# A decoder layer's last batch attended in two halves of 256 tokens, with half of its routing beside the attention

## The reference

```python
def _relu_kernel(x, proj):                      # random features, M = 128
    return relu(einsum('blhd,md->blhm', x, proj) / sqrt(128)) + 1e-3
q, k, v = query @ Wq, source @ Wk, source @ Wv  # 16 heads of 64; source: 77 context tokens a batch
kvs = einsum('blhm,blhd->bhmd', kp, v)
num = einsum('blhm,bhmd->blhd', qp, kvs)
den = einsum('blhm,bhm->blh', qp, sum_l(kp))
att = num / den ; out = einsum('blhd,hdk->blk', att, Wo)
...
routing = softmax(xf @ router_w.T)              # 8 experts, the best 2 of each token
y = (silu(xf @ w_gate) * (xf @ w_up)) @ w_down  # hidden size 256
out = sum over the 2 of weight * y
```

## Time and profile before

| | |
|---|---|
| median of 3 runs | 296.51 us (294.48 to 297.17) |
| the profiled execution | 296.67 us, its span 294.9 us |
| mixer and folds | to about 108 us |
| attention (PE) | to 195.3 us |
| experts (PE) | 196.6 to about 280 us |
| busy | PE 84%, PEld 71%, DVE 62%, ACT 54%, POOL 37% |
[...]

### The profile page before, as it was taken

The page is one execution under the profiler, slowest core; times in us unless marked ns, Lnnn a source line. Parts: engine busy times, 40 slices in busy tenths (PEclk is TensorE's granted clock), DMA queues, the critical chain, the costliest instruction groups (busy, mean ns, idle before and its releaser), DMA issues.

```text
span 294.9 us, 5862 instructions
## 1 busy us (share of the span) xinstructions
PE 247.8 (84%) x1730; PEld 210.3 (71%) x1730; DVE 182.7 (62%) x721; ACT 158.2 (54%) x339; POOL 108.7 (37%) x161
## 2 busy tenths in 40 slices
PE   7799999999899999998999899859587777788800
PEld 3468786767789998996899688748576766777700
DVE  2867877878288878977796889687521212112206
ACT  3275565646677776776576766514444424345400
POOL 4388623402010010074006503614565655655520
PEclk9999999999999999999999999999999999999955
DMA  7899669999120000010001100537857885672147
GB/s 241 248 216 182 110 135 186 170 181 190 48 111 0 2 0 4 0 47 28 1 2 36 38 2 13 160 94 232 226 159 213 201 235 167 174 209 75 32 139 288
DMA packets 36254, 35.36 MB, mean 120 GB/s; under 512 B 3973, under 2 KB 27658, under 8 KB 36096
## 3 DMA queue, kind: packets, MB, share of 16 engines
q1 hardware_dynamic: 33520, 30.23, 44.6%
q0 software_dynamic: 2272, 4.24, 4.2%
q10 hardware_dynamic: 432, 0.52, 0.5%
HBM read 19.84 MB, written 14.32 MB: 116 GB/s over the span
## 4 chain that ended last, share of the span: by engine, by line
PE 64%; DVE 13%; issue 8%; DMA 5%; ACT 4%; POOL 2%; another core or an unknown queue 2%; SPq 1%; POOLq 0%; DVEq 0%; ACTq 0%
PE num L1455 15%; PE front L1559 9%; PE num L1569 5%; PE front L1399 5%; PE num L1377 4%; PE front L280 4%; PE front L282 3%; PE front L281 3%; DVE X L1033 3%; PE back L1341 2%; PE num L280 2%; PE back L1288 2%; DVE X L1279 2%; DVE hid L1247 2%
## 5 line engine op out<-in xcount | busy, mean ns | idle before, releaser
L1033 DVE SCALAR_TENSOR_TENSOR X<-num,rden,X 128x128 f32<-128x128 f32 x256 | 75.6, 342 | 4.8
L1455 PEld LDWEIGHTS num<-kvw_sb,q 128*128 128x128 f32 x512 | 66.7, 190 | 14.0 <-issue 5.7
L1455 PE MATMUL num<-kvw_sb,q 128*128 128x130 f32 x512 | 69.1, 277 | 6.1 <-DVE X L1033 5.7
L589 POOL DMA_INDIRECT dispatched<-rows,slot_i x32 | 31.3, 977 | 56.1 <-PE front L282 28.9
L744 ACT ACTIVATE relu_z<-front 128x512 f32<-128x512 f32 x64 | 38.1, 595 | 24.2 <-PE front L282 22.5
L1247 DVE TENSOR_TENSOR hid<-front,silu_g 128x256 f32<-128x256 f32 x39 | 16.5, 423 | 55.1 <-ACT silu_g L774 38.7
L624 POOL DMA_INDIRECT expert_out<-yo,xb x39 | 38.0, 975 | 32.0 <-ACT yo L778 19.4
L1559 PE MATMUL front<-xT,wgu_sb 128*128 128x128 f32 x312 | 41.8, 277 | 5.2 <-issue 3.6
L640 ACT ACTIVATE q<-relu_z 128x512 f32<-128x512 f32 x64 | 40.4, 632 | 5.9 <-PE num L1455 0.4
L1559 PEld LDWEIGHTS front<-xT,wgu_sb 128*128 128x128 f32 x312 | 37.9, 192 | 6.2 <-issue 6.2
L1569 PE MATMUL num<-wd_sb,hid 128*128 x156 | 25.8, 288 | 10.8 <-DVE hid L1247 9.4
(11 more groups left out here) (175 smaller groups left out, 382.2 us busy)
## 6 DMA issues: line engine op xcount, KB each, us to landing
wgu_sb<-in_wgu SPq DMA_DIRECT2D x39, 256.0 KB
dispatched<-pad_row SPq DMA_DIRECT2D x3, 2795.0 KB, 19.1
xb<-dispatched SPq DMA_DIRECT2D x39, 65.0 KB
y_back<-expert_out SPq DMA_DIRECT2D x4, 512.0 KB, 5.0
wd_sb<-in_wd SPq DMA_DIRECT2D x1, 1024.0 KB, 4.8
out<-X SPq DMA_DIRECT2D x4, 256.0 KB, 2.2
X<-in_x SPq DMA_DIRECT2D x3, 256.0 KB, 4.7
expert_out<-yo,xb POOLq DMA_INDIRECT x39
```

What stands on the lines that cost most here:

```text
L589: g.indirect_dma_start(out=xs, out_offset=bass.IndirectOffsetOnAxis(ap=slot_i[:, m % 2, t, k:k + 1], axis=0), in_=rows[:, m % 2, k, t, :], ...
L1033: ins = v.scalar_tensor_tensor(tile_of(n, t), banks[:, t // 2, t % 2, 0:P], rden[:, f % 2, t:t + 1], tile_of(n, t), ALU.mult, ALU.add)
L1455: last = nc.tensor.matmul(num[:, 2 * (h % 2) + t // 2, HA * (t % 2):HA * (t % 2 + 1)], q[:, h % 4, part], kvw_h, start=True, stop=True)
```

## The change

The last batch is worked in two halves of its tokens. A unit is now two heads for 256 tokens instead of one head for 512: `features` issues 3 matmuls of 256 columns for each of the two heads into the halves of the same bank, `numerators` uses the first head's keys for two tiles and the second's for the other two, and DVE adds both heads to the same two tiles, so that the third and fourth update of X wait for the first and second. After 8 units, tokens 0 to 255 have all their heads. Routing has five jobs now: batches 0 to 2 whole, and the two halves (`HALF_A`, `HALF_B`) of batch 3. The first half's routing is placed beside units 8 to 12 of the last batch on DVE, 11, 12 and 14 on PE, and 11, 14 and 15 on ACT; the second's stays between the first blocks of the experts, with half the tokens. The functions take slices of the tiles; counts of steps follow the width of the job (`routed`).

Scatters: `SPREAD` lists, for each batch in progress and job, the half heads at which one is issued. Batch 0 sends two in batch 1 and six in batch 2, four halves apart; batch 1 sends two in batch 2 and six in batch 3; batch 2 sends eight in batch 3 at halves 19 to 30, and the first half of the last batch four at 31, 33, 35 and 37. The experts keep four scatters, at gates 4 to 7, and with the last gate at 7 the sends of blocks 3 to 38 spread over 31 blocks instead of 28.

```diff
-        SCATTER_HEAD = (10, 13)
-        PACE = (0, 1, 3, 5, 6, 8, 9, 11)
+        SPREAD = {(1, 0): (26, 30), (2, 0): (2, 6, 10, 14, 18, 22), (2, 1): (26, 30), (3, 1): (1, 5, 9, 12, 15, 17),
+                  (3, 2): (19, 20, 22, 23, 25, 27, 28, 30), (3, 3): (31, 33, 35, 37)}
+        NORM_AT, HALF_NORM_AT = 2, 4
         BURST = 3
-        BURST_GATES = (4, 5, 6, 7, 7, 8, 9, 10)
+        BURST_GATES = (4, 5, 6, 7)
         HALVES = 2
         ACT_Y3, ACT_TWICE, ACT_SECOND = (5, 6), (5, 8), (8, 10)
         PE_Y3, PE_LOGITS, PE_RANKS = (5, 6), (6, 7), (8, 10)
         PE_SUMS, DVE_SUMS = 1, 3
         DVE_TABLE = (5, 3)
-        ROUTE_STEPS = 21
+        JOBS = [(m, 0, TPB) for m in range(NB - 1)] + [(NB - 1, 0, TPB // 2), (NB - 1, TPB // 2, TPB)]
+        HALF_A, HALF_B = NB - 1, NB
+        PE_HALF, ACT_HALF, DVE_HALF = (11, 12, 14), (11, 14, 15), 8
...
+        def heads_summed(r):
+
+            return (JOBS[r][0] + 1) * H - (H // 2 if r == HALF_A else 0)
...
-            def scatters(n, m):
-
-                first = 2 * SCATTER_HEAD[m < NB - 2]
-                for i in range(TOPK * TPB):
-                    after_head(n, first + PACE[i])
-                    scatter(m, i // TOPK, i % TOPK)
+            sent_of = [0] * len(JOBS)
+
+            def scatters(n, r, start=0, stop=None):
+
+                for half in SPREAD.get((n, r), ())[start:stop]:
+                    after_head(n, half)
+                    scatter(r, sent_of[r])
+                    sent_of[r] += 1
 
             for n in range(1, NB):
                 if n == 1:
                     ln2(NB - 1)
+                scatters(n, n - 2, 0, NORM_AT)
                 third_norm(n - 1)
-                scatters(n, n - 1)
-            third_norm(NB - 1)
+                scatters(n, n - 2, NORM_AT)
+                if n < NB - 1:
+                    scatters(n, n - 1)
+            scatters(NB - 1, NB - 2, 0, HALF_NORM_AT)
+            third_norm(HALF_A)
+            scatters(NB - 1, NB - 2, HALF_NORM_AT)
+            scatters(NB - 1, HALF_A)
+            third_norm(HALF_B)
 
             def last_scatters():
-                for i in range(TOPK * TPB):
+                for i in range(TOPK * width(HALF_B)):
                     pool.wait_ge(gu_full, BURST_GATES[i])
-                    scatter(NB - 1, i // TOPK, i % TOPK)
+                    scatter(HALF_B, i)
...
+            def turned_rows(r):
+                act.wait_ge(tb_full, r + 1)
+                copy(y3T[:, 0:P * width(r)], t_bank[:, 0:P * width(r)]).then_inc(y3T_done, 1)
...
+                        if k == ACT_HALF[0]:
+                            turned_rows(HALF_A)
+                        if k == ACT_HALF[1]:
+                            second_silu(HALF_A)
+                        if k == ACT_HALF[2]:
+                            second_rows(HALF_A)
...
-                    ins = v.scalar_tensor_tensor(tile_of(n, t), banks[:, t // 2, t % 2, 0:P], rden[:, f % 2, t:t + 1], tile_of(n, t),
+                    tile = tile_of(n, t if n < NB - 1 else 2 * (h // (H // 2)) + t % 2)
+                    if n == NB - 1 and t >= 2:
+                        dve.wait_ge(pair_step if t == 2 else att_done, h + 1 if t == 2 else f * HALVES + 1)
+                    ins = v.scalar_tensor_tensor(tile, banks[:, t // 2, t % 2, 0:P], rden[:, f % 2, t:t + 1], tile,
                                                  ALU.mult, ALU.add)
                     if t % 2:
                         ins.then_inc(att_done, 1)
-
...
+                    elif n == NB - 1 and t == 0:
+                        ins.then_inc(pair_step, 1)
...
+                if r >= HALF_A:
+                    dve.wait_ge(ln3_step, 2 * (r + 1))
+                    v.tensor_tensor(l_diff[:, part], l_diff[:, part], rstd[:, part], ALU.mult).then_inc(u_done, 1)
+                    dve.wait_ge(u_done, 2 * (r - HALF_A) + 2)
...
-                if (1, 2) <= (k, t) <= (2, 1):
-                    third_norm(m, TPB * k + t - TPB - 2)
+                if (1, 3) <= (k, t) <= (2, 2):
+                    third_norm(m, TPB * k + t - TPB - 3)
...
+                at = TPB * (k - DVE_HALF) + t
+                if at == 0:
+                    third_stats(HALF_A, 0)
+                    third_stats(HALF_A, 1)
+                if at == 1:
+                    third_moments(HALF_A, 0)
+                    third_moments(HALF_A, 1)
+                if at == 2:
+                    mean_share(HALF_A)
+                if at == 8:
+                    centred_logits(HALF_A)
+                    tops(HALF_A)
+                if at == 9:
+                    top_indices(HALF_A)
+                    top_number(HALF_A)
+                if at == 10:
+                    choose(HALF_A)
+                    take(HALF_A)
+                if at == 11:
+                    difference(HALF_A)
+                    never_zero(HALF_A)
+                if at == 12:
+                    inverse(HALF_A)
+                    third_norm(HALF_A, 0)
+                if at == 13:
+                    third_norm(HALF_A, 1)
+                if at == 16:
+                    slots(HALF_A)
+                    slots_chosen(HALF_A)
+                if at == 17:
+                    places(HALF_A)
+                    second_weight(HALF_A)
+                    counts(HALF_A)
+                if at == 18:
+                    first_weight(HALF_A)
+                    place_numbers(HALF_A)
...
+            def head_of(n, h, i):
+
+                return h if n < NB - 1 else 2 * (h % (H // 2)) + i
+
             def features(n, h):
                 wait_past(pe, relu_done, n * H + h - 1)
+                if n == NB - 1:
+                    tokens = slice(POS // 2 * (h // (H // 2)), POS // 2 * (h // (H // 2) + 1))
+                    for i in range(2):
+                        part = slice(M * head_of(n, h, i), M * (head_of(n, h, i) + 1))
+                        last = split_matmul(z_bank[h % 2][:, POS // 2 * i:POS // 2 * (i + 1)], feat_hi[:, part], feat_lo[:, part],
+                                            y2T_hi[:, n, tokens], y2T_lo[:, n, tokens])
+                    last.then_inc(z_full, 1)
+                    return
                 part = slice(M * h, M * (h + 1))
                 split_matmul(z_bank[h % 2], feat_hi[:, part], feat_lo[:, part], batch(y2T_hi, n), batch(y2T_lo, n)
                              ).then_inc(z_full, 1)
...
             def numerators(n, h):
                 f = n * H + h
                 pe.wait_ge(q_done, f + 1)
-                kvw_h = batch(kvw_sb[:, :, HA * h:HA * (h + 1)], n)
                 for t in range(TPB):
                     part = slice(P * t, P * (t + 1))
                     if t % 2 == 0:
                         wait_past(pe, att_done, (f - 2) * HALVES + t // 2 + 1)
-                    last = nc.tensor.matmul(num[:, 2 * (h % 2) + t // 2, HA * (t % 2):HA * (t % 2 + 1)], q[:, h % 4, part], kvw_h,
-                                            start=True, stop=True)
+                    at = head_of(n, h, t // 2)
+                    last = nc.tensor.matmul(num[:, 2 * (h % 2) + t // 2, HA * (t % 2):HA * (t % 2 + 1)], q[:, h % 4, part],
+                                            kvw_sb[:, n, HA * at:HA * (at + 1)], start=True, stop=True)
                 last.then_inc(num_done, 1)
...
+            def turn_last(r):
+
+                pe.wait_ge(att_done, heads_summed(r) * HALVES)
+                transposes(t_bank, [X[:, TPB * (NB - 1) + t, :] for t in range(*JOBS[r][1:])]).then_inc(tb_full, 1)
...
+                        if k == PE_HALF[0]:
+                            turn_last(HALF_A)
+                        if k == PE_HALF[1]:
+                            router_logits(HALF_A)
+                        if k == PE_HALF[2]:
+                            ranks(HALF_A)
...
-                    turn_last()
+                    turn_last(HALF_B)
                 if s == 1:
-                    router_logits(NB - 1)
+                    router_logits(HALF_B)
 
             pipeline(pe, [(0, turn_x), (1, gate_up), (1, behind_gate), (2, down)], next_experts, beside={
-                3: [lambda: ranks(NB - 1)]},
+                3: [lambda: ranks(HALF_B)]},
```

More of the change, by code:

```diff
@@ L326, in turned_x, with width, tiles_of, tiles_routed @@
             return (t_bank, o_bank)[s][:, 0:P] if s < 2 else tx_bank[j % 2][:, 0:P]
+        def width(r):
+            return JOBS[r][2] - JOBS[r][1]
+        def tiles_of(r):
+            return slice(JOBS[r][1], JOBS[r][2])
+        def tiles_routed(r):
+            return sum(width(j) for j in range(r + 1))
+        def heads_summed(r):
+            return (JOBS[r][0] + 1) * H - (H // 2 if r == HALF_A else 0)
+        def routed(r, step=None):
+            steps = [2 * width(j) + 13 for j in range(r + 1)]
+            if step is None:
+                return 1 + sum(steps)
+            return 1 + sum(steps[:r]) + (step if step == 0 else width(r) if step == TPB else step - 2 * TPB + 2 * width(r))
```

(23 more changed lines are left out.)

249 lines of the change are left out of this document (124 added, 125 removed).

## The result

The changed kernel takes 289.05 us (median of 4 runs, 286.90 to 289.92) where the kernel before takes 296.84 (4 runs, 294.48 to 299.05): a ratio of 0.9746, interval 0.9695 to 0.9798, so it is faster by 2.5%. The profiled execution took 288.63 us, its span is 286.9 against 294.9.

The account below looks back on a forecast made before the run. PE was taken to lead the chain, DVE to bound dense routing, with stalls from dense indirect DMAs. Terms -2.6 + 2.7 + 1.6 - 1.3 - 0.7 - 1.9 = -2.2 against 296.67 gave 294.5 us, range 288.5 to 300.5.

Parts of the forecast that it names:

- the sum: Whole kernel: all terms added, -2.2 us against the profiled execution, 294.5 us; chance 0.44 for 291.5 to 297.5.
- rival B: Experts: spacing pays there too, only the 5 blocks with doubled sends stall, -6.4 us, 290 us; chance 0.22.
- (b): Last batch: the first half's routing moves into DVE's attention work, 3.1 us of it against 0.44 idle: +2.7 us.
- (c): Last batch, POOL: twelve scatters at its minimum distance, priced at two stalls: +1.6 us, bounds -1.6 and +5.3.
- (d): Block 0 of the experts: batch 2's last scatter comes earlier, so PE's wait for `xb` goes: -1.3 us.
- (e): PE's routing between the first expert blocks halves: -0.7 us.
- (f): Experts: four scatters leave, at 0.46 us a DMA: -1.9 us, or 0 if only PE's own work counted.
- (a): Scatters of batches 0 and 1: lone ones stall nobody, so PE's two waits go: -2.6 us, bounds 0 and -2.6.
- (g): Last batch's feature matmuls at 256 columns: 0 taken, upper bound +7.7 us if a load is not hidden.
- (h): Last batch, DVE: the third update's wait for the first costs 0, upper bound +3.2 us.
- C: Stalls follow the number of DMAs, not their density; all 71 stay, (a) is lost: 297.1 us; chance 0.14.
- D: Slower: the last batch pays the experts' 0.46 us for each of 18 DMAs: 299.6 us, 302 where (a) fails; chance 0.20.

Follow-up runs that it names:

- half late: The changed kernel with the first half's last four scatters put back into the experts and the sends over 28 blocks: 273.16 us, ratio 0.9989 to the kernel before.
- singles: The kernel before with only the scatters of batches 0 and 1 spread singly: 275.19 us, ratio 1.0014, then 274.48 us, 0.9972.
- units: The kernel before with only the last batch's two-head units, 256-column features and pair waits: 272.48 us, ratio 0.9945.
- old pace: The changed kernel with the experts' sends over 28 blocks from gate 11: 272.70, 272.33 and 272.68 us, ratios 0.9969, 0.9935 and 0.9956 to the kernel before.
- one each: The changed kernel with the four expert scatters beside blocks 5, 7, 9, 11 and one send per block: 275.83 us, ratio 1.0055 to the kernel before.

## Why the prediction was right, and where it was not

The direction was open in it (0.38 faster) and 289.05 lies in the range, near its lower end. The likeliest case, the sum of 294.5, was 5.4 us too high; rival B, "spacing pays in the experts too", had 290 with a chance of 0.22. It is B that put the measured time into the range.

Where the sum went wrong shows when its terms are laid on the stretches. It has -2.2 us against the profiled execution before, and -8.0 were measured: 5.8 are missing. Batches 1 and 2 hold 1.3 of them (-2.6 foretold, -3.9 measured), the last batch up to the first silu 1.1 (terms (b), (c) and (d) +3.0, measured +1.9), the experts 4.1 (terms (e) and (f) -2.6, measured -6.7); the start-up and the end take 0.6 off. The step that failed most is (f), the price of the experts' DMAs. That the last batch comes within 1.1 us of its three terms is partly luck: (b) was 0.75 us too small and (c), up to the last reciprocal, 3.9 too large. By its own steps:

- **(a) Lone scatters stall nobody: right, and too small.** -2.6 was taken, the two stretches measure -3.9 (-2.02 and -1.86) and are down to what they take where nothing stalls (27.96 and 29.12 us against 27.97 and 29.10). The waits of PE, 2.56 us in all, do not show all of a stall; where the other 1.4 us stand was not followed up.
- **(b) The first half's routing on DVE: right in kind, too small.** +2.7 against 3.45 (29.10 less 25.65, scatters without effect by *half late* and *singles*). The work itself was priced right: DVE is busy 26.26 us in that batch against 23.20 in *units*, 3.06 more where the prediction has 3.1. What failed is the 0.44 us of DVE's idle time that the routing was to fill. The idle time did not shrink, it grew from 2.45 to 2.84 us.
- **(c) A second visible stall in the last batch: wrong.** +1.6 was taken, for two stalls against one, with -1.6 as the lower bound. The kernel before lost 2.32 us there (27.82 against 25.50) and the changed one loses 0.01 (29.11 against 29.10), so up to the last reciprocal the term is -2.3, outside its bounds. The twelve scatters did not stand as the prediction had them, all at POOL's least distance: four do (177.16 to 180.95), the next four stand up to 1.88 us apart, and of the first half's four two start behind the last reciprocal. Those four again stand at the least distance, and the loss of 2.15 us beside their end falls to block 0, outside (c)'s stretch. One of the two foretold stalls came, there. One dense group of four cost nothing and another stood beside a loss, so density alone doesn't say when a stall comes.
- **(d) Block 0's rows.** -1.3. The `xb` wait went as foretold, and PE starts block 0's gate 3.75 us sooner, 1.5 us of it by its distance to the last reciprocal. But four dense scatters now end at block 0, and up to the first silu the stretch is 0.65 longer. Where nothing stalls the same stretch is 3.06 shorter (4.33 to 1.27), which is about what (b) costs. There the change is a trade of two equal things: from batch 3's first reciprocal to the first silu 29.83 us before and 30.37 after.
- **(e) The routing in the experts.** -0.7. It lies around and behind the first silu and can't be told from (f) in these traces.
- **(f) Four scatters fewer in the experts: mis-sized.** -1.9, or -2.6 with (e), against -6.7. Rival B's reckoning, 17 us x 5/8 left, fits the size: 17.1 us lost before, 10.0 to 11.8 after. Its premise, that only doubled sends stall, is not shown. What the numbers do say is that a fixed price for each DMA isn't enough. The stretch holds 44 indirect DMAs before and 40 after, a loss of 0.39 us each before and 0.25 to 0.30 after.
- **(g), (h)**: 0 taken, 0.15 measured. The load is hidden at 256 columns: the two groups of three matmuls take 0.44 and 0.36 us, 0.12 to 0.15 each, with loads whose records of 0.19 us lie under the matmuls', not the 0.21 each of the upper bound, whose +7.7 us is refuted.
- **C, the number decides: refuted.** All 71 indirect DMAs stay, and in batches 1 and 2 nothing is left of the loss; batch 2's stretch holds eight scatters in either kernel and loses 1.94 us before and 0.02 after. **D** had the last batch pay the experts' price for 18 DMAs. 14 of them start before the last reciprocal, at a loss of 0.01, and the 2.15 us behind it are far from its 8.3.

**What stays open.** Why the slower chip stalls behind dense indirect DMAs and three others do not; that it lies in the delivery of semaphores was the author's reading, and no run shows it. Whether it is the chip or something that was so at that time is open too. Should the two traces of the result come from unequal conditions, a part of the difference would be theirs; no run rules that out. Where the 0.4% of the quicker chips lies is not shown either: by the two traces of one chip the changed kernel's experts are no shorter (62.88 against 62.50 us). In the experts, how the gain of the slower chip divides between the wider spacing and the fewer scatters: *singles*, *old pace* and *one each* were made to tell, but all ran on chips on which there is nothing to divide. The claim that density is what counts rests on the two traces of the slower chip, with the quicker ones for what the same work takes undisturbed, and not on an edit of one part there.

## What to carry to other kernels

Where several engines wait for each other and none is late by its own work, take the length of the stretch from a trace without the disturbance, if any chip gives one, and not from the single wait that the timeline names; here PE's two named waits, 2.56 us, held two thirds of the 3.95 lost in batches 1 and 2, and a third wait that looked the same, 1.08 us, was no stall at all. Work moved beside attention is paid at the engine that sets its end (3.45 us of DVE here) and has to buy as much behind it. A gain that comes from stalls avoided holds for the chip that stalls. This change gave 2.5% on one and 0.4% on two others, and there spacing still further (*one each*) cost 2.45 us.

## What the runs showed of the hardware that was not expected

- One kernel takes 296.8 us in the result's runs and 274.1 to 274.7 on three chips; the granted clock is 1.00 in batches 1 to 3 of both. The instructions' own records are as long (an update of X 342 and 343 ns on average, a scatter 977 and 976); what differs in batches 1 and 2 is waits beside runs of GpSimd's indirect DMAs, at the second of the earlier trace rows 1.23 us of PE, 2.58 of DVE, 2.04 of ACT and 1.29 of POOL.
- In the experts the DMAs move 179 GB/s on average on the slower chip and 226 on a quicker one, in proportion to the lengths of 79.61 and 62.50 us: the same bytes in another time.
- A row number that SP reads costs its queue about 0.29 us, an estimate from 14 of them fewer, with which the group went from 6.57 to 2.46 us. Moving these reads behind the loads that were waited for was worth 1.13 us of the kernel.
